# A graph network on one core: the node rows' moments computed again in the last edge pass, the table that carried them taken out, and table rows of 272 numbers

## The reference

```python
h = jnp.maximum(_layernorm(x, axis=-1), 0.0)
x = x + _L2_gnn_ref(h, edge_attr_64, edge_index, ...)      # gives x3
h = jnp.maximum(_layernorm(x, axis=-1), 0.0)
x = x + _L3_gnn_ref(h, edge_index, edge_weight, ...)

def _L3_gnn_ref(x, edge_index, edge_weight, W, b, gamma, beta):
    ...
    norm = dinv[row] * dinv[col] * ew
    h = x @ W + b
    out = jax.ops.segment_sum(norm[:, None] * h[row], col, num_segments=n)
    mean = jnp.mean(out, axis=0)
    var = jnp.mean(jnp.square(out - mean), axis=0)
    out = (out - mean) * jax.lax.rsqrt(var + BN_EPS) * gamma + beta
    return jax.nn.relu(out)
```

## Time and profile before

| | |
|---|---|
| median of 3 runs | 3142.06 us (3127.89 to 3143.46) |
| the profiled execution | 3136.22 us, of which the span of the trace is 3134.4 us |
| busy over the span | PE 2077.7, DVE 2139.2, ACT 1682.8, POOL 1582.2 us |
| granted TensorE clock, mean | 0.833 |

### The profile page before, as it was taken

The page is one execution under the profiler, slowest core; times in us unless marked ns, Lnnn a source line. Parts: engine busy times, 40 slices in busy tenths (PEclk is TensorE's granted clock), DMA queues, the critical chain, the costliest instruction groups (busy, mean ns, idle before and its releaser), DMA issues. The chain is left out here.

```text
span 3134.4 us, 48304 instructions
## 1 busy us (share of the span) xinstructions
PE 2077.7 (66%) x10165; PEld 1475.8 (47%) x10165; DVE 2139.2 (68%) x8782; ACT 1682.8 (54%) x4590; POOL 1582.2 (50%) x1489
## 2 busy tenths in 40 slices
PE   3673534637767778788745788777776666664665
PEld 1332512525545656666632334343335655564555
DVE  5798523338877888898857777777745544444999
ACT  2592101238874656565647988898965444442222
POOL 3200565520007888888827666655607777774000
PEclk9896767879996677666767999999998888877999
DMA  2497422449997787787747999999966555554998
GB/s 72 146 360 304 80 56 75 101 114 323 322 306 264 243 249 230 244 255 234 235 103 216 290 290 286 283 294 286 292 170 216 178 186 181 181 175 137 316 316 280
DMA packets 494677, 696.59 MB, mean 222 GB/s; under 512 B 66363, under 2 KB 357398, under 8 KB 485932
## 3 DMA queue, kind: packets, MB, share of 16 engines
q1 hardware_dynamic: 416414, 511.30, 51.5%
q0 software_dynamic: 63360, 130.75, 15.6%
q10 hardware_dynamic: 14736, 52.96, 4.7%
HBM read 394.91 MB, written 327.18 MB: 230 GB/s over the span
## 5 line engine op out<-in xcount | busy, mean ns | idle before, releaser
L274 POOL DMA_INDIRECT xs<-x_d,table_src x400 | 386.7, 967 | 350.1 <-DVE x L1502 128.4
L274 POOL DMA_INDIRECT xs<-n_d,srcI x200 | 240.1, 1201 | 325.6 <-DVEq L1151 270.4
L274 POOL DMA_INDIRECT xd<-n_d,dstI x200 | 235.4, 1177 | 60.9 <-issue 54.5
L274 POOL DMA_INDIRECT xd<-x_d,table_dst x200 | 211.4, 1057 | 65.1 <-issue 64.5
L1860 PE MATMUL bank<-xs,same 128*128 128x129 f32 x400 | 109.2, 363 | 180.7 <-ACT sums L1829 93.0
L1721 POOL DMA_INDIRECT r_d<-rd,out_row x200 | 196.5, 982 | 60.9 <-issue 60.9
L1657 PEld LDWEIGHTS bank<-nmsg,same 128*128 128x128 f32 x400 | 61.4, 193 | 267.7 <-ACT sums L1589 209.0
L1657 PE MATMUL bank<-nmsg,same 128*128 128x128 f32 x400 | 99.9, 333 | 130.2 <-ACT sums L1589 74.9
L269 ACT ACTIVATE root<-tmp,eps 128x4 f32<-128x4 f32 (+3 forms) x253 | 76.8, 303 | 196.4 <-DVE tmp L245 195.8
L250 DVE RECIPROCAL rs<-root 128x4 f32<-128x4 f32 (+3 forms) x253 | 51.9, 205 | 185.5 <-ACT root L269 173.2
L474 POOL DMA_INDIRECT sum_d<-add,to x40 | 62.5, 1563 | 228.4 <-ACT add L663 187.7
(11 more groups left out here) (393 smaller groups left out, 7131.5 us busy)
## 6 DMA issues: line engine op xcount, KB each, us to landing
n_d<-T SPq DMA_DIRECT2D x98, 528.0 KB, 3.8
nt<-n_d SPq DMA_DIRECT2D x49, 1056.0 KB, 7.3
r<-r_d SPq DMA_DIRECT2D x98, 520.0 KB, 5.5
bc<-dst_d SPq DMA_DIRECT2D x170, 256.0 KB, 4.6
r_d<-nv SPq DMA_DIRECT2D x49, 528.0 KB, 7.7
v_d<-nv SPq DMA_DIRECT2D x49, 528.0 KB, 7.7
nv<-v_d SPq DMA_DIRECT2D x49, 528.0 KB, 4.3
x_d<-x SPq DMA_DIRECT2D x100, 256.0 KB, 4.8
```

The costliest lines, as they stand in the source:

```text
L274: pool.indirect_dma_start(out=out, out_offset=None, in_=table, in_offset=bass.IndirectOffsetOnAxis(ap=index, axis=0)).then_inc(s, 16)
```

## The change

The table `v_d` goes. In the MLP stage v is still computed and stored into `r_d`, and the second store is left out. The convolution stage computes v of the nodes once more for the moments: SP loads a chunk of x3 and of the node constants `meta_d` (the factor is in column M_Q) in place of the chunk of `v_d`; DVE takes the statistics of 8 x 128 more rows per step (`nodes_stats`), and `rs`, `nb` and the sums between have 16 columns where they had 8; DVE weighs the factors (`weigh_nodes`) and copies the two last columns (`node_tails`); ACT makes v in two halves of four instructions (`nodes_v(0)`, `nodes_v(1)`), placed between the segment sums; PE's `node_moments` move from lag 2 to lag 3. Rows of `r_d` get 272 numbers for 260 (1,088 bytes for 1,040), with 12 more zeros at the end, so the store of v writes 576 bytes a row for 528, the scatter 1,088 for 1,040, and the output stage loads 544 KB a chunk for 520.

```diff
-RW = 260
+RW = 272
+VW = RW - D
-        v_d = dram("v_d", (NN, TW))
 # MLP stage
-            nv = sb("nv", [P, 4, B, TW], F32, c)
+            nv = sb("nv", [P, 4, B, VW], F32, c)
                     def store_v(g, s):
                         sp.wait_ge(nv_ready, g + 5)
-                        sp.dma_start(chunk_of(r_d, g, D, TW), nv[:, s % 4, :, :]).then_inc(nv_stored[s % 4], 16)
-                        sp.dma_start(chunk_of(v_d, g, 0, TW), nv[:, s % 4, :, :]).then_inc(nv_stored[s % 4], 16)
+                        sp.dma_start(chunk_of(r_d, g, D, VW), nv[:, s % 4, :, :]).then_inc(nv_stored[s % 4], 16)
-                    nc.vector.memset(nv[:, :, :, D + 2:TW], 0.0)
+                    nc.vector.memset(nv[:, :, :, D + 2:VW], 0.0)
...
 # convolution stage: SP
                     def load_nodes(g, s):
                         sp.wait_ge(nodes_done, g + 1)
-                        sp.dma_start(nv[:, s % 4, :, :], v_d[bass.ds(g * (B * P), B * P), :].rearrange("(p j) f -> p j f", p=P)).then_inc(
-                            nv_in[s % 4], 16)
+                        sp.dma_start(nx[:, s % 4, :, :], chunk_of(x3_d, g, D)).then_inc(n_in[s % 4], 16)
+                        sp.dma_start(nm[:, s % 4, :, :], chunk_of(meta_d, g, 8)).then_inc(n_in[s % 4], 16)
 # convolution stage: DVE
+                    weigh_nodes = weighting(slice(2 * G, norms), lambda g, s: nm[:, s % 4, :, M_Q], n_weighted, 0)
+                    def nodes_stats(g, s):
+                        dve.wait_ge(n_in[s % 4], count4(g, s, 2))
+                        for j in range(B):
+                            last = nc.vector.bn_stats(st[:, s, 2 * G + j, :], nx[:, s % 4, j, :])
+                        last.then_inc(n_summed, 1)
+                    def node_tails(g, s):
+                        nc.vector.tensor_copy(nv[:, s % 4, :, D:D + 2], nm[:, s % 4, :, M_Q:M_BARE + 1]).then_inc(node_tails_ready, 1)
-                    pipeline(dve, NGE, [(inverse, 2), (weigh, 2), (own, 5), (weighed, 2), (offset, 2), (stats, 1), (kept, 5), (sames, 2), (rows_summed, 1),
-                                        (differences, 1), (tails, 2), (squares, 1), (total, 1)], S8)
+                    pipeline(dve, NGE, [(inverse, 2), (weigh, 2), (weigh_nodes, 2, -1), (own, 5), (weighed, 2), (nodes_weighed, 2, -1), (offset, 2),
+                                        (stats, 1), (nodes_stats, 1, -1), (kept, 5), (sames, 2), (rows_summed, 1), (nodes_summed, 1, -1),
+                                        (differences, 1), (tails, 2), (node_tails, 1, -1), (squares, 1), (total, 1)], S8)
 # convolution stage: ACT
+                    def nodes_v(half):
+                        def part(g, s):
+                            act.wait_ge(scaled, g + 1)
+                            for j in range(half * G, half * G + G):
+                                last = nc.scalar.activation(nv[:, s % 4, j, 0:D], nx[:, s % 4, j, :], ACT.Relu,
+                                                            bias=nb[:, s, 2 * G + j:2 * G + j + 1], scale=rs[:, s, 2 * G + j:2 * G + j + 1])
+                            last.then_inc(nv_ready, 1)
+                        return part
-                    pipeline(act, NGE, [(total(0), 3), (total(1), 3), (relus, 2), (total(2), 3), (total(3), 3), (roots, 1)], S8)
+                    pipeline(act, NGE, [(total(0), 3), (nodes_v(0), 2, -1), (total(1), 3), (relus, 2), (total(2), 3), (nodes_v(1), 2, -1),
+                                        (total(3), 3), (roots, 1)], S8)
 # convolution stage: PE
                             if j == 0:
-                                pe.wait_ge(nv_in[s % 4], count4(g, s))
+                                pe.wait_ge(nv_ready, g * 2 + 2)
+                                pe.wait_ge(node_tails_ready, g + 1)
-                    pipeline(pe, NGE, [p for j in range(G) for p in ((total(j), 3), (moments(j), 7), (node_moments(j), 2, -1))], S8)
+                    pipeline(pe, NGE, [p for j in range(G) for p in ((total(j), 3), (moments(j), 7), (node_moments(j), 3, -1))], S8)
```

More of the change, by code:

```diff
@@ L1456, in _ @@
                         sp.wait_ge(nx_stored[s], 32 * ((NGE - 1 - s + 3) // 4) + 32)
-                        sp.wait_ge(nv_stored[s], 32 * ((NGE - 1 - s + 3) // 4) + 32)
+                        sp.wait_ge(nv_stored[s], 16 * ((NGE - 1 - s + 3) // 4) + 16)
                 @block.vector
@@ L1476, in _ @@
                         dve.sem_inc(nx_stored[s], 32)
-                        dve.sem_inc(nv_stored[s], 32)
+                        dve.sem_inc(nv_stored[s], 16)
                     def stats(g, s):
@@ L1511, in nodes_h2 @@
                         dve.wait_ge(scaled, g + 1)
-                        dve.wait_ge(nv_stored[s % 4], count4(g, s, 2))
+                        dve.wait_ge(nv_stored[s % 4], count4(g, s))
                         for j in range(BD):
@@ L1593, in nodes_h2 @@
                         act.wait_ge(scaled, g + 1)
-                        act.wait_ge(nv_stored[s % 4], count4(g, s, 2))
+                        act.wait_ge(nv_stored[s % 4], count4(g, s))
                         for j in range(BD, B):
@@ L1669, in build @@
             B = 2 * G
+            norms = 2 * G + B
+            nx = sb("nx", [P, 4, B, D], F32, c)
+            nm = sb("nm", [P, 4, B, 8], F32, c)
             nv = sb("nv", [P, 4, B, TW], F32, c)
[L1671 to L1675, removed]
+            n_summed, n_weighted, node_tails_ready, nv_ready, nodes_done = (sem(f"gc_{n}") for n in (
+                "n_summed", "n_weighted", "node_tails_ready", "nv_ready", "nodes_done"))
+            n_in = [sem(f"gc_n_in{s}") for s in range(4)]
+            st = sb("st", [P, S8, norms, 6], F32, c)
+            tmp = sb("tmp", [P, 2, 3, norms], F32, c)
+            root, rs, nb = (sb(n, [P, S8, norms], F32, c) for n in ("root", "rs", "nb"))
             bc = sb("bc", [P, 4, G * P], F32, c)
@@ L1695, in count8, with count4, chunk_of @@
                 return (g - s) * (2 * dmas) + 16 * dmas
-            def count4(g, s):
-                return (g - s % 4) * 4 + 16
+            def count4(g, s, dmas=1):
+                return (g - s % 4) * (4 * dmas) + 16 * dmas
+            def chunk_of(table, g, width):
+                return table[bass.ds(g * (B * P), B * P), 0:width].rearrange("(p j) f -> p j f", p=P)
             with nc.Block() as block:
@@ L1781, in weighed, with nodes_weighed, nodes_summed @@
                         dve.wait_ge(weighted, g + 1)
+                    weigh_nodes = weighting(slice(2 * G, norms), lambda g, s: nm[:, s % 4, :, M_Q], n_weighted, 0)
+                    def nodes_weighed(g, s):
+                        dve.wait_ge(n_weighted, g + 1)
+                    def nodes_stats(g, s):
[3 more added lines that the diff above has]
+                        last.then_inc(n_summed, 1)
+                    def nodes_summed(g, s):
+                        dve.wait_ge(n_summed, g + 1)
+                    def node_tails(g, s):
+                        nc.vector.tensor_copy(nv[:, s % 4, :, D:D + 2], nm[:, s % 4, :, M_Q:M_BARE + 1]).then_inc(node_tails_ready, 1)
                     def tails(g, s):
```

2 lines of the change are left out of this document (1 added, 1 removed).

## The result

The changed kernel takes **3149.05 us** (median of 13 runs, 3141.47 to 3154.7), the kernel before, run beside it, 3141.47 (13 runs, 3127.89 to 3148.22). The ratio is 1.0026, with a 95% interval of 1.0016 to 1.0036: slower by 8 us, inside the 0.5% that was called no change. The profiled execution took 3141.47 us, its span is 3139.6; it is the fastest of the 13, so its trace shows 5 us of difference to the trace of before where the medians show 7.6.

A forecast was written before the change was run, and what follows sets the result against it. The ACT-DVE ring was taken to bound the MLP stage, POOL the convolution stage, DVE the output stage. Terms -1.5 + 0.7 + 2 + 10.7 + 1.5 = +13.4 us on 3136.2 gave 3150 us, range 3136 to 3167.

The forecast's parts named there:

- MLP steady step: MLP stage: the ring ACT, DVE, ACT has no transfer in it, so steady steps keep 13.10 us.
- MLP relief: MLP stage: dropping the second store of v shrinks only late starts, -1.5 us, bounds nothing and -12.
- Rival B: Faster: relieved DMA queues free the MLP stage's back edges and filling, -12 us, sum 3130 us; chance 0.12.
- Memsets: Larger zeroed pad ahead of the first gather in both stages: 0.35 us more each, +0.7 us.
- Convolution, steady: Convolution stage: ACT's step becomes 9.0 us, hidden under POOL's 10.3; slowed transfers add 2 us in all.
- the lock: Convolution stage: DVE instructions with two SBUF inputs slow POOL's transfers, 0.04 us a group, 2 us in all, at most 17.
- Filling: Convolution stage while it fills: longer ACT and DVE steps delay gather 8 by 10.7 us, bounds 7 and 14.
- root 5 to third sum: Convolution filling: ACT's way from root of group 5 to the third sum takes 7.1 us, where it was 5.28: +1.8.
- Root 0: Convolution filling: root of group 0 comes 1.65 us later, behind the eight node statistics.
- Output stage: Output stage: wider rows load 24 KB more a chunk, DVE still sets the pace, +1.5 us, bounds -2 and +10.
- C: Markedly slower: ACT's convolution step exceeds 10.3 us, so POOL waits in every step, 3171 us; chance 0.1.
- D: Output stage bound by its queues (+10) or POOL stopped as by the upper bound: 3158 to 3168 us; chance 0.18.

The follow-up runs named there:

- e1: Changed kernel with the second store of v put back into the MLP stage, in pieces of one row: 3162.76 us, 1.0088 of the kernel before.
- e10: Changed kernel with rows of 260 and the second store back in one unbroken piece: 3150.75 us, 1.0035 of the kernel before.
- e9: Kernel before with POOL's wait split, so gathers wait for segment sums and only SP's load for the moments: 3137.67 us, 0.9988 of the kernel before.
- e12: The changed kernel unchanged, run again on a second chip: 3149.19 us, 1.0020 of the kernel before.
- e2: Changed kernel with table rows of 260 numbers again instead of 272: 3143.55 us, 1.0022 of the kernel before.
- e3: Changed kernel without ACT's eight instructions on node rows in the convolution stage: 3141.39 us, 1.0007 of the kernel before.
- e4: Changed kernel with POOL's wait split, so gathers wait for segment sums and only SP's load for the moments: 3133.09 us, 0.9992 of the kernel before.

## Why the prediction was right, point by point

The time (3150 for 3149.05) was met better than its terms deserve. It was built as +13.4 us on an execution of 3136.2; measured are +7.6 us on a median of 3141.47. The base was 5 us low and the sum 6 us high, and the two errors cancelled: that the time was met to 1 us is luck. The range (3136 to 3167) also holds no change at all, so it is the terms, and not the time, that test the reasoning; the largest, the filling, was worked out from its chain and came out within 2 us.

- **MLP steady step: right.** In the changed kernel ACT goes from root to root in 13.09 us with the same wait on the offsets as in the earlier trace rows:
```profile
1934.64 0.31 ACT L269 ACTIVATE root<-tmp,eps 128x24 f32<-128x24 f32 x1
1936.63 2.03 ACT L1595 ACTIVATE nv<-nx,nb,rs 128x128 f32<-128x128 f32 x5 [1.04 <-DVE nb L261]
...
1947.73 0.31 ACT L269 ACTIVATE root<-tmp,eps 128x24 f32<-128x24 f32 x1
```
- **MLP relief: the mis-sized term,** -1.5 predicted, -5.4 measured (mean of nine profiles), inside the bounds. The step that failed: "the ones at the back edges name no transfer", hence worth nothing. They name none, and yet they shorten without the second store and lengthen when it is broken (e1): the excess of the steps at the back edges was 11.2 us before and 4.6 after, and the sets with and without the store are 2.8 us apart at the nearest (e10). The bound was also priced by ACT's stop alone: at the stop of 2.38 us the step was 3.7 us longer. Rival B's mechanism was real, at less than half its size. The changed kernel's longest stop of this kind, for the 2.38 us of the earlier trace rows:
```profile
1907.30 0.60 ACT L1566 ACTIVATE hsT<-bank 128x512 f32<-128x512 f32 x1 [1.04 <-issue]
```
- **Memsets: right.** The pad takes 0.43 us for 0.11, +0.32 for 0.35:
```profile
2336.34 0.43 DVE L1764 MEMSET rd<- 128x448 f32 x1
```
- **Convolution, steady: the step right, the lock too high.** Steps of 9.02 us where 9.0 were worked out; POOL never waits for them. The +2 for transfers slowed beside two-input instructions is not there: 461.1 and 461.3 us without the change (before, e9), 460.1 to 461.9 in the eight kernels with it, mean 461.1, and the gathers' mean fell (969 ns for 977). The rule of the Trainium skill that the prediction weighed (page "SBUF — State Buffer", section "Who interferes with whom") speaks of an exclusive lock on the port pair that DVE and GpSimd share; some 0.3 us more of such instructions in each group (2.9 us for 2.6) left no trace that these runs can show.
- **Filling: right in mechanism, 1 to 2 us short.** +12.9 us in the trace of the change, +12 over the five kernels with its code, for 10.7. Five steps took 41.39 (41.1 predicted), root 5 to third sum 7.08 (7.1): exact. Root 0 came 15.82 us after the first gather for 12.85, +3.0 for 1.65, but the term itself was right: from DVE's first statistics to root 0 it is 2.52 us before and 4.19 after. The other 1.3 us passed ahead of them, waiting for the gathered rows. Before, then after:
```profile
2358.52 0.87 DVE L1769 BATCH_NORM_STATS2 st<-xs 128x6 f32<-128x128 f32 x4 [11.22 <-DMA xs<-x_d,table_src]
```
```profile
2350.07 0.87 DVE L1775 BATCH_NORM_STATS2 st<-xs 128x6 f32<-128x128 f32 x4 [12.52 <-DMA xs<-x_d,table_src]
```
  That start lies 10.33 us behind the first gather before, 10.39 to 11.72 in the five kernels with the same code and 10.83 in e9 without it, so it can't be told from scatter. The last hand-over, third sum to gather 8, took 2.80 us for 2.18, and that isn't owed to the change either: it is 2.17 or 2.18 in e12, e1, e2 and e10, whose PE has the same work. There the granted clock over those 2 to 3 us is 0.88 to 1.00; in the profile of the change it is 0.58 (2402.70 to 2405.60 us), and two matmuls that take 0.39 us in e12 take 0.64. Scatter 0 started 42.3 us after the first gather, predicted near 40. e3 and e4 confirm the chain: without ACT's part 7 to 8 of the 12 us go, without the wait for the moments 9 to 10.
- **Output stage: right.** +2 for +1.5. Over 180 us the changed kernel moves 322 GB/s at a DMA share of 0.94, the kernel before 318 GB/s at 0.94, so the wider rows came at no more busy time of the DMA engines; over all profiles it is 317 to 325 GB/s at 0.93 to 0.96 with rows of 272, 316 to 319 at 0.94 or 0.95 with 260. That agrees in direction with the rule cited from the Trainium skill (page "DMA: Bandwidth & Descriptors", section "How a descriptor splits into AXI transactions"), by which rows on the 256-byte grid waste less.
- **The rivals.** C (ACT above 10.3 us a step) is out: 9.02. D is out by its price, +2 us in the output rows for +10, though its sign was nearly there: DVE waited 4.6 us in the output stage, and 5.0 and 5.7 in e3 and e1, where over 5 was to tell. B gave 5.4 us in the MLP stage but not the rest.

The measured columns add up, by their means, to -5.4 + 12.1 - 0.1 + 1.9 = +8.5 us, with 0.3 more of memset ahead of them, against +7.6 and +6.6 of the two medians.

## What to carry to other kernels

Work that an engine has room for in the steady loop is still paid for once, while the pipeline fills, if the engine that sets the pace later is idle there: price an addition by the filling steps, not by the busy shares. A wait that guards two buffers at once makes the slower reader of one hold up the writer of the other; asked for each buffer alone, it gave back 9 to 10 of the 12 us, but on the chip where ACT starts late it cost 3%, so such an edit is to be timed on more than one chip. And before undoing an edit as an experiment, see that the undone part is the old one down to the shape of its transfers: one store in pieces of a row turned a question of 5 us into an answer of 14.

## What was not expected of the hardware

- The stops at loop back edges change with one store more or less although the profile names no releaser: ACT's are 1.5 to 2.4 us in the kernel before, 2.2 to 5.0 in e1 with its broken store, and none of the changed kernel's reaches 1.3. The share of the DMA engines goes the same way (0.98, 1.04 and 0.85 from 1800 to 1900 us); what links the two no run shows. In the convolution stage DVE stops at its own back edge. In the changed kernel it starts on a root 4.5 us after ACT has finished it (2532.49), stops again for 2.04 us, and ACT stands still for 8.34 us behind it:
```profile
2532.18 0.31 ACT L269 ACTIVATE root<-tmp,eps 128x16 f32<-128x16 f32 x1 [1.74 <-DVE tmp L245]
...
2537.02 0.25 DVE L250 RECIPROCAL rs<-root 128x16 f32<-128x16 f32 x1 [4.87 <-issue]
...
2539.73 1.14 DVE L1822 SCALAR_TENSOR_TENSOR rd<-sums,rg_dst,rd 128x129 f32<-128x129 f32 x4 [2.04 <-issue]
```
```profile
2540.99 1.65 ACT L1869 ACTIVATE nv<-nx,nb,rs 128x128 f32<-128x128 f32 x4 [8.34 <-DVE nb L261]
```
  One step of ACT in eight is then 12.8 to 15.5 us; the 1.3 us that each step is shorter than POOL's 10.3 pays it back, so POOL never saw it.
- Two Trainium2 chips differed by 10% on the same program (3142 and 3452 us), in the stages that gather rows, with ACT held up by something that its trace doesn't name. Their granted clocks differ too, 0.83 and 0.78 to 0.79; which is cause and which effect is open.
